# Two 256-element biases loaded as rows and turned into columns on TensorE, with four identity transposes fewer in front

## What is computed

```python
def _L0_xattn_ref(query, input_flatten, input_padding_mask, Wq, bq, Wk, bk, Wo, bo):
    Q = query @ Wq.T + bq
    K = input_flatten @ Wk.T + bk
    scores = jnp.einsum('nhqd,nhkd->nhqk', Q, K)          # one head of 256
    scores = jnp.where(input_padding_mask[:, None, None, :], -jnp.inf, scores)
    attn = jax.nn.softmax(scores, axis=-1)
    out = jnp.einsum('nhql,nhld->nhqd', attn, V)           # V is input_flatten
    return out @ Wo.T + bo
x = x + tanh(g_xattn) * _L0_xattn_ref(_layernorm(x), ctx_1024, mask, Wq, bq, Wk, bk, Wo, bo)
x = x + tanh(g_ffn) * clip((_layernorm(x) @ sign(weights).T) * scale + bias, -100, 100)
```

## Time and profile before

| what | value |
|---|---|
| time, median of 3 runs | 79.76 us (79.69 to 80.13) |
| time of the profiled execution | 79.95 us |
| span of the profiled execution | 77.9 us |
| PE busy | 71.5 us (92%) |
| DVE busy | 55.7 us (71%) |
| POOL busy | 52.6 us (68%) |
| ACT busy | 37.2 us (48%) |
| packets of queue q1 and q10 | 7232 and 474 |

### The profile page before, as it was taken

The page is one execution under the profiler, slowest core; times in us unless marked ns, Lnnn a source line. Parts: engine busy times, 40 slices in busy tenths (PEclk is TensorE's granted clock), DMA queues, the critical chain, the costliest instruction groups (busy, mean ns, idle before and its releaser), DMA issues.

```text
span 77.9 us, 1590 instructions
## 1 busy us (share of the span) xinstructions
PE 71.5 (92%) x534; PEld 65.9 (85%) x534; DVE 55.7 (71%) x164; ACT 37.2 (48%) x100; POOL 52.6 (68%) x98
## 2 busy tenths in 40 slices
PE   2999599999999999999999999999999989899920
PEld 2998597996799999989998999899999979778600
DVE  2397865892269759938992998479669656999940
ACT  0064239567559508551944494176509454603030
POOL 6005783989603805889999999899999999734300
PEclk9999999999999999999999999999999999999997
DMA  0799999990000000012003000300030030040025
GB/s 19 249 356 359 352 349 347 350 322 1 0 4 0 0 0 8 0 62 77 0 4 135 0 8 0 135 0 0 0 135 0 8 110 24 0 135 0 0 76 193
DMA packets 7714, 7.44 MB, mean 95 GB/s; under 512 B 792, under 2 KB 7451, under 8 KB 7707
## 3 DMA queue, kind: packets, MB, share of 16 engines
q1 hardware_dynamic: 7232, 7.21, 28.3%
q10 hardware_dynamic: 474, 0.14, 0.8%
HBM read 5.25 MB, written 2.10 MB: 94 GB/s over the span
## 4 chain that ended last, share of the span: by engine, by line
PE 81%; DMA 4%; DVE 3%; POOL 3%; ACT 3%; issue 2%; DVEq 0%; POOLq 0%
PE ps_Z L562 16%; PE ps_K L562 15%; PE ps_S L624 9%; PE ps_F L562 8%; PE ps_O L643 8%; PE ps_xT L557 5%; PE ps_x1T L557 4%; PE ps_cT L557 4%; DMA wq_sb<-in_L_xattn_Wq_dram 4%; PE ps_S L632 2%; POOL xn L310 1%; PE ps_S L619 1%; PE ps_x1T L739 1%; PE ps_x1T L737 1%; ACT K_sb L212 1%
## 5 line engine op out<-in xcount | busy, mean ns | idle before, releaser
L409 DVE SCALAR_TENSOR_TENSOR x_sb<-ps_O,recip_p,xb_sb 128x256 f32<-128x256 f32 x14 | 6.1, 479 | 9.5 <-PE ps_O L643 9.5
L322 POOL TENSOR_TENSOR xb_sb<-x_sb,bo_g 128x256 f32<-128x256 f32 x16 | 11.3, 730 | 1.3 <-ACT bo_g L249 1.3
L202 ACT CAST cT_hi<-ps_cT 128x512 fp32r<-128x512 f32 x8 | 4.7, 586 | 13.5 <-PE ps_cT L557 13.4
L328 POOL TENSOR_TENSOR f_biased<-f_scaled,bi_g 128x256 f32<-128x256 f32 x12 | 8.6, 740 | 3.2 <-DVE f_scaled L417 3.1
L310 POOL TENSOR_SCALAR xn<-x_sb,rstd_x,off_x 128x256 f32<-128x256 f32 x16 | 9.9, 627 | 0.5
L562 PE MATMUL ps_Z<-woT_hi,cT_hi 128*128 128x256 f32 x32 | 9.7, 304 | 0.0
L562 PE MATMUL ps_K<-cT_hi,wqk_hi 128*128 128x256 f32 x32 | 9.1, 284 | 0.0
L562 PE MATMUL ps_K<-cT_hi,wqk_lo 128*128 128x256 f32 x32 | 9.0, 282 | 0.0
L562 PE MATMUL ps_K<-cT_lo,wqk_hi 128*128 128x256 f32 x32 | 9.0, 282 | 0.0
L562 PE MATMUL ps_Z<-woT_lo,cT_hi 128*128 128x256 f32 x32 | 9.0, 280 | 0.0
L562 PE MATMUL ps_Z<-woT_hi,cT_lo 128*128 128x256 f32 x32 | 9.0, 280 | 0.0
(11 more groups left out here) (144 smaller groups left out, 207.8 us busy)
## 6 DMA issues: line engine op xcount, KB each, us to landing
x_sb<-in_x_dram SPq DMA_DIRECT2D x8, 256.0 KB, 5.9
ctx_sb<-in_ctx_dram SPq DMA_DIRECT2D x8, 256.0 KB, 6.2
out_dram<-out_sb SPq DMA_DIRECT2D x7, 256.0 KB, 2.1
wq_sb<-in_L_xattn_Wq_dram SPq DMA_DIRECT2D x1, 256.0 KB, 3.1
wk_sb<-in_L_xattn_Wk_dram SPq DMA_DIRECT2D x1, 256.0 KB, 3.5
wo_sb<-in_L_xattn_Wo_dram SPq DMA_DIRECT2D x1, 256.0 KB, 4.6
w_sb<-in_L_ffn_weights_dram SPq DMA_DIRECT2D x1, 256.0 KB, 5.0
out_dram<-out_sb SPq DMA_DIRECT2D x1, 128.0 KB, 1.7
```

The lines of the kernel that those rows point to most:

```text
L322: nc.gpsimd.tensor_tensor(xb_sb[:, r], x_sb[:, r], bo_g[:], ALU.add).then_inc(xb_done, 1)
L328: nc.gpsimd.tensor_tensor(f_biased[:, r], f_scaled[:, r], bi_g[:], ALU.add).then_inc(f_biased_done, 1)
L409: nc.vector.scalar_tensor_tensor(out=x1_sb[:, r], in0=ps_O[:, b], scalar=recip_p[:, r:r + 1], in1=xb_sb[:, r], op0=ALU.mult, op1=ALU.add). ...
```

## The change

bq and bk are loaded as single rows of 256 elements on one partition. PE turns them into columns: for each bias and each half a product of a strided slice of the row (1 x 128, the stationary side) with a single 1.0, into four columns of the bank `ps_O`. These four products stand in PE's program behind the eighth of the identity transposes (`BIAS_AFTER = 7`, counted from 0), and six more transposes follow, 14 in all instead of 18. DVE reads the columns from the bank: `bq_d` is now scaled from there, and `bk_col` is a copy. Both stand ahead of `wq_sum` now, behind one wait for the products (`ps_bias_ready`).

```diff
-WARM_UP = 18
+WARM_UP = 14
+BIAS_AFTER = 7
...
-            act.dma_start(bq_col[:], bq.rearrange("(p c) -> p c", c=DC)).then_inc(bq_loaded, 16)
-            act.dma_start(bk_col[:], bk.rearrange("(p c) -> p c", c=DC)).then_inc(bk_loaded, 16)
+            act.dma_start(bq_row[:], row(bq)).then_inc(bq_loaded, 16)
+            act.dma_start(bk_row[:], row(bk)).then_inc(bk_loaded, 16)
...
+            dve.wait_ge(ps_bias_ready, 1)
+            nc.vector.tensor_scalar(bq_d[:], o_bank[:, 0:DC], 1.0 / D, None, ALU.mult).then_inc(bq_d_done, 1)
+            nc.vector.tensor_copy(bk_col[:], o_bank[:, DC:2 * DC]).then_inc(bk_col_ready, 1)
             dve.wait_ge(wq_loaded, 16)
             nc.vector.tensor_reduce(wq_sum[:], wq_sb[:], AX.X, ALU.add).then_inc(wq_sum_done, 1)
-            dve.wait_ge(bq_loaded, 16)
-            nc.vector.tensor_scalar(bq_d[:], bq_col[:], 1.0 / D, None, ALU.mult).then_inc(bq_d_done, 1)
...
-            for _ in range(WARM_UP):
+            for n in range(WARM_UP):
                 nc.tensor.transpose(ps_x1T[:, 0, 0:P], ident[:], ident[:])
+                if n == BIAS_AFTER:
+
+                    pe.wait_ge(bq_loaded, 16)
+                    pe.wait_ge(bk_loaded, 16)
+                    for k, v in enumerate((bq_row, bk_row)):
+                        for c in range(DC):
+                            last = nc.tensor.matmul(o_bank[:, DC * k + c:DC * k + c + 1],
+                                                    v[:, :].rearrange("o (p c) -> o c p", c=DC)[:, c], ones_1[:, 0:1],
+                                                    start=True, stop=True)
+                    last.then_inc(ps_bias_ready, 1)
...
-            pe.wait_ge(bk_loaded, 16)
+            pe.wait_ge(bk_col_ready, 1)
```

More of the change, by code:

```diff
@@ L97, in gated_xattn_ffn @@
         wq_sb, wk_sb, wq2 = sb("wq_sb", [P, DC, D]), sb("wk_sb", [P, DC, D]), sb("wq2", [P, DC, D])
-        bq_col, bk_col = sb("bq_col", [P, DC]), sb("bk_col", [P, DC])
+        bq_row, bk_row, bk_col = sb("bq_row", [1, D]), sb("bk_row", [1, D]), sb("bk_col", [P, DC])
         bq_d, wq_sum, wq_add = sb("bq_d", [P, DC]), sb("wq_sum", [P, DC]), sb("wq_add", [P, DC])
@@ L129, in gated_xattn_ffn @@
                              "sel_done", "mask_ready"))
+        ps_bias_ready, bk_col_ready = sem("ps_bias_ready"), sem("bk_col_ready")
         bq_d_done, wq_sum_done, wq_add_done, wq2_ready, ps_wqk_ready, wqk_hi_ready, wqk_lo_ready = (
```

## The result

| | before | after |
|---|---|---|
| median of 4 runs each | 79.83 us (79.69 to 80.13) | 82.43 us (81.77 to 82.88) |
| ratio, 95% interval | | 1.0304 (1.0261 to 1.0346) |
| profiled execution, its span | 79.95, 77.9 us | 82.22, 80.3 us |
| packets of q10 | 474 | 190 |

The changed kernel is 3.0% slower, 2.4 us. The direction was forecast; the size, 80.6 us in a range up to 81.9, was not.

A forecast was written before the change was run, and what follows sets the result against it. The DVE and POOL chain to the first `ps_xT` was taken to bound the kernel. DVE's wait of +0.88 less 0.08 for `bq_d` gave +0.8 us, 80.6 us on the median; range 80.1 to 81.9.

The forecast's parts named there:

- The bound: PE runs nearly without a gap from the first `ps_xT` at 9.40 us, so the end moves with that start.
- The early clock: At the start, PE runs at 1.2 GHz before 5.2 us, although the clock column says 1.00.
- The rows land by 3.3: Loads on ACT's queue: bk's row issued at 1.02, landing at 3.3 us, with ends 2.6 and 4.6.
- Eight passes in 1.2 us: Bias products on PE behind the eighth transpose: 1.2 us, columns ready at 4.5; 2.0 if weight loads doubled.
- The way into DVE: From PE's last product: 0.04 to DVE, 0.14 for two operations, `wq_sum` at 4.68 against 3.80, +0.88 us.
- bq_d off the chain: DVE between `wq_sum` and `wq_add`: without `bq_d` behind `wq_sum` the chain gets 0.08 us shorter.
- Four transposes: worth nothing as long as the clock rises: Start of PE: removing four transposes changes nothing, as PE waits for `wq2` anyway, if the clock rises as before.
- rival 2: PE's clock stays at 1.2 GHz longer, chance 0.1: 81.8 us if it rises half way (1.2 more), at worst 83.1.
- Three quarters of the stretch are still transposes: PE's first stretch: the argument against the clock staying low for longer, which had chance 0.1.
- PE itself is not in it: Chain up to `ps_xT` at 9.40: only DVE and POOL instructions set it; PE fills time with transposes until 5.2.
- Rivals 1 and 2: Rival 1: bias columns much later, by late row or slower weight loads, 81.1 to 82.2 us, chance 0.2; rival 2: 0.1.
- Rival 3's gain: Loads: without 8-byte packets wq and x(0) land up to 0.4 us earlier, time 79.5; no loss or gain, chance 0.12.

The follow-up runs named there:

- e2: Kernel before with 14 transposes and four unused products, 1 row x 1 column, behind the eighth; DVE and column loads as before: ratio 1.0203.
- e10: Kernel before with 14 transposes and the same unused products behind the eighth, but of 128 rows x 1 column: ratio 1.0181.
- e9: Kernel before, column loads, no products: bq_d and a bk copy ahead of wq_sum, waiting for the seventeenth of 32 transposes: ratio 1.0175.
- e1: Kernel before with 14 identity transposes instead of 18 and nothing else: ratio 1.0011.
- e13: Kernel before with 14 transposes and unused products of 1 row x 128 columns behind the eighth: ratio 1.0256.
- e11: Kernel before with 14 transposes and unused full products, 128 rows x 128 columns, behind the eighth: ratio 1.0010.
- e14: Changed kernel with full products, from bias rows laid into zeroed tiles of 128 partitions, identity as moving side: ratio 1.0300 to the kernel before.
- e4: Kernel before without the two bias loads, bq and bk set to zero by GpSimd: ratio 1.0059.
- e8: Kernel before with only bk as a row, its products behind the first products of wk and wq2, copied behind the first statistics: ratio 1.0036.
- e12: Both biases as rows, bq's products behind the second of 14 transposes, bk's behind wk's and wq2's first products, wq_sum first: ratio 1.0037 to before.
- e3: Changed kernel with wq_sum put back ahead of the wait for the bias columns: ratio 1.0212 to the kernel before.
- e6: Changed kernel with 128 columns of ones instead of one as the products' moving side, on one row: ratio 1.0271 to the kernel before.
- e7: Changed kernel with 17 transposes instead of 14, filling PE's idle time ahead of wk's products: ratio 1.0314 to the kernel before.
- e5: Changed kernel with the four products behind all 14 transposes instead of behind the eighth: ratio 1.0546 to the kernel before.

## Why the prediction was wrong

Step by step, against the profile after:

- **The bound.** Right. The first `ps_xT` sets the end; it moved 2.36 us and the span 2.4.
- **The early clock.** Right that PE starts at 1.2 GHz in spite of a clock column of 1.00.
- **The rows land by 3.3.** Too pessimistic and harmless: q10's four packets for both rows are over by 3.0, although bk's row was issued at 1.27 and not at 1.02. PE's products start at 3.41 (forecast 3.3) behind the eighth transpose, as they do at 3.40 in e2, where they wait for no row.
- **Eight passes in 1.2 us: this term failed.** They took 1.87. "The weight load costs 0.05 to 0.06 at either level" was drawn from a transpose's first load and carried over to float32 products. The eight passes step by 0.213 (1.86 us in e2 too, 1.71 in e10 with `kbias`'s own shape), twice the 0.11 of `kbias`: at 1.2 GHz the whole pass takes twice as long, and what stands unhidden ahead of a first transpose did not tell of it. The page's formula, 107 ns for 128 columns ("TensorE: Matmul & The Clock Gate", section LDWEIGHTS, of the Trainium skill), names no clock level; the trace agrees at 2.4 GHz (steps of 0.11) and shows twice that at 1.2 GHz. The other value that the prediction weighed, 2.0, was the nearer one.
- **The way into DVE.** Right: 5.28 to `bq_d` at 5.31, and 0.14 to `wq_sum` at 5.45. So +1.65 instead of +0.88.
- **bq_d off the chain.** -0.17 instead of -0.08: `wq_add` follows `wq_sum` by 0.71 instead of 0.88. Together +1.48, shown alone by e9 as 1.4 us of time.
- **"Four transposes: worth nothing as long as the clock rises".** The transposes are worth nothing (e1), but the clock did not rise: rival 2, given 0.1. Its half-way price was 1.2, measured 0.95 at `ps_xT`. Its reason, thin passes, is shown by e2, e10 and e13 against e11. "Three quarters of the stretch are still transposes" was no protection. With it failed "PE itself is not in it", carried over from the chain before: at 1.2 GHz PE's own program was the last to reach `ps_xT`, 0.95 us behind `xn`.
- **The chances.** Rivals 1 and 2 were priced as if one excluded the other. They came together: 0.68 more of DVE's wait, from passes at twice the price, and 0.95 on top. They are two effects: in e11 and e14 full products step by 0.213 as well, and the clock is up for the context transposes all the same. Each alone would have lain inside the range: the first is e9 with 1.0175, 81.2 us; the second is 80.6 + 0.95 = 81.6, an estimate. Both together did not.
- **Rival 3's gain.** wq did land earlier, 3.5 (2.8 after its issue) against 3.78; but x(0) did not, so the 79.5 of the small-packet rule ("DMA: Bandwidth & Descriptors", Specifications, of the Trainium skill) was not to be had: without any small packets (e4) the time was 0.6% longer.

## What to carry to other kernels

Before a product is put into TensorE's first microseconds, price it at the clock of that place, read from the steps of its neighbours there, and not from the same product later on. Eight passes of thin products (one row or one column) ahead of the clock's rise cost twice here: their own length at the low level, and a low clock for what followed; full ones of the same length in the same place cost nothing where nobody waited for them (e11). And rivals that can come true together need a price for both at once.

## What the runs showed of the hardware

- The clock rose behind 14 full transposes and a short idle time (e1), and behind full products (e11), but late with 1 x 1, 1 x 128 and 128 x 1 products in the same place (e2, e13, e10), although the profile calls PE busy for 3.69 of 3.70 us from 1.50 to 5.20 in each of these and in the change, and for 3.25 in e1. By the steps between PE's passes (0.21 at one level, 0.11 at the other) the rise lay between 4.6 and 7.8 us in all eight profiles without eight thin passes at the start (before, e1, e4, e8, e9, e11, e12, e14), between 8.5 and 10.9 in the change, e2, e3, e6, e7, e10 and e13, and behind 14 in e5. The Trainium skill ("TensorE: Matmul & The Clock Gate", Part 4) says that the full clock does not engage for transposes. Here it rose with nothing but float32 transposes ahead of it, in the kernel before and in e1; the measurement decides. Where in a run it rises moves from execution to execution, so small differences between e2, e10 and e13 are not read.
- With both column loads of 8-byte packets, x(0) landed 3.5 to 3.8 us after its issue in seven profiles (before, e1, e2, e9, e10, e11, e13); with one of them, 4.0 (e8); with rows or no bias loads at all, 3.8 to 5.6 in eight (the change 5.0, e3 4.4, e4 5.6, e5 5.1, e6 3.8, e7 4.3, e12 4.8, e14 4.2; those of e4 and e5 are their kernels' longest executions). With the small packets wq comes a little later (2.8 to 3.1 after issue with both column loads, 2.5 to 2.9 without) and yet the loads behind it are steadier. Why stays open; no run tests it.
- A row of 1 KB was fast in a queue that had nothing before it: in the changed kernel q10 moved two packets by 1.8, 1.1 us after bq's row was issued at 0.73, and two more by 3.0, 1.7 us after bk's at 1.27. Rows issued later, under full load, had taken 2.3 to 3.6 us.
